# Reordering edits in the attention stage of a one-core transformer block: fill transfers spread over more turns, one GpSimd wait dropped, filler matmuls and two VectorE steps moved

## What is computed

```
xn = layernorm(x) * g_in
q  = xn @ Wq (16 heads of 64);  k, v = xn @ Wkv (one head, shared)
s  = q k^T / 8 + attn_bias[h];  causal mask; rows of the key mask; one extra "null" key per head
o  = softmax(s) v;  y = layernorm(o @ Wo) * g_out
n  = rmsnorm(y) * norm_w;  logits = n @ router^T + router_b
each of 16 experts takes its 512 best tokens: gelu(n W1 + b1) W2 + b2, weighted and scattered
out = x + that
```

## Time and profile before

| what | value |
|---|---|
| median of three executions | 1998.95 us (1996.95 to 2002.93) |
| the profiled execution | 2002.93 us, of which 2001.2 us lie between its first and last instruction |
| mean granted TensorE clock | 0.985 of full speed |
| PE busy | 1910.4 us (95%) |
| DVE, ACT, POOL busy | 1509.1, 1319.0, 1226.7 us |
| DRAM traffic | 139 GB/s over the span |

### The profile page before, as it was taken

One profiled execution on the slowest core, in us unless ns is written; L12 is line 12 of the kernel. 1 busy time (PEld: TensorE's weight loads), 2 busy tenths in 40 slices (PEclk: granted clock), 3 DMA queues, 4 the chain that ended last, 5 costly groups with the idle time before them and its releaser, 6 DMA issues.

```text
span 2001.2 us, 42090 instructions
## 1 busy us (share of the span) xinstructions
PE 1910.4 (95%) x12660; PEld 1702.7 (85%) x12660; DVE 1509.1 (75%) x2361; ACT 1319.0 (66%) x2624; POOL 1226.7 (61%) x1229
## 2 busy tenths in 40 slices
PE   4799999998789999999999999999999999999998
PEld 3678888877779898898999899898998889988897
DVE  5778887776887878777787877777787777777764
ACT  4667777754556666666676666767666666766664
POOL 3478888873057647565674757656574756657561
PEclk9899999998999999999999999999999999999999
DMA  6844444334743525254343525344352525434342
GB/s 247 320 139 128 125 131 139 106 97 171 231 107 112 138 100 142 95 147 106 125 125 112 142 95 142 97 140 123 113 147 90 152 87 150 106 122 120 121 126 44
DMA packets 90255, 263.14 MB, mean 131 GB/s; under 512 B 20593, under 2 KB 22353, under 8 KB 85073
## 3 DMA queue, kind: packets, MB, share of 16 engines
q1 hardware_dynamic: 70866, 211.44, 32.3%
q0 software_dynamic: 17024, 34.19, 9.0%
q10 hardware_dynamic: 2304, 16.78, 2.1%
HBM read 223.47 MB, written 55.60 MB: 139 GB/s over the span
## 4 chain that ended last, share of the span: by engine, by line
PE 69%; DVE 3%; ACT 2%; issue 1%; DMA 0%; POOL 0%; DVEq 0%; ACTq 0%; POOLq 0%
PE experts_b_a L2313 18%; PE experts_b_y L252 11%; PE experts_b_y L253 11%; PE experts_b_y L254 11%; PE experts_b_b L2313 9%; PE experts_b_c L2313 4%; PE experts_b_turn L2293 1%; ACT experts_h L1814 1%; DVE experts_x_lo L1967 1%; PE experts_b_c L2302 1%; PE experts_b_turn L2302 1%; PE experts_b_c L2391 0%; ACT experts_y_out L1748 0%; DVE experts_y_out L2005 0%; DVE experts_y_out L2103 0%
## 5 line engine op out<-in xcount | busy, mean ns | idle before, releaser
L252 PE MATMUL experts_b_y<-experts_w_hi,experts_h_hi 128*128 128x512 f32 x1024 | 406.3, 397 | 0.0
L1592 POOL TENSOR_TENSOR experts_s_raw<-experts_w_raw 128x256 f32<-128x256 f32 x128 | 147.7, 1154 | 421.7 <-DMA experts_w_raw<-in_w 410.7
L253 PE MATMUL experts_b_y<-experts_w_lo,experts_h_hi 128*128 128x512 f32 x1024 | 404.2, 395 | 0.0
L254 PE MATMUL experts_b_y<-experts_w_hi,experts_h_lo 128*128 128x512 f32 x1024 | 399.1, 390 | 0.0
L2313 PE MATMUL experts_b_a<-experts_x_hi,experts_w_hi 128*128 (+1 forms) x1024 | 290.2, 283 | 9.2 <-ACT experts_p_copy L1773 7.0
L2313 PE MATMUL experts_b_a<-experts_x_hi,experts_w_lo 128*128 (+1 forms) x1024 | 290.0, 283 | 0.0
L2313 PE MATMUL experts_b_a<-experts_x_lo,experts_w_hi 128*128 (+1 forms) x1024 | 289.9, 283 | 0.0
L254 PEld LDWEIGHTS experts_b_y<-experts_w_hi,experts_h_lo 128*128 128x128 f32 x1024 | 192.4, 188 | 43.3
L2313 PEld LDWEIGHTS experts_b_a<-experts_x_hi,experts_w_hi 128*128 128x128 f32 x1024 | 194.8, 190 | 29.5 <-issue 11.4
L252 PEld LDWEIGHTS experts_b_y<-experts_w_hi,experts_h_hi 128*128 128x128 f32 x1024 | 194.3, 190 | 24.0
L253 PEld LDWEIGHTS experts_b_y<-experts_w_lo,experts_h_hi 128*128 128x128 f32 x1024 | 194.3, 190 | 21.2
(11 more groups left out here) (378 smaller groups left out, 5564.7 us busy)
## 6 DMA issues: line engine op xcount, KB each, us to landing
experts_w_raw<-in_w SPq DMA_DIRECT2D x256, 512.0 KB, 3.3
bias<-in_bias SPq DMA_DIRECT2D x68, 256.0 KB, 4.1
xn_dram<-wq_hi ACTq DMA_DIRECT2D x16, 1024.0 KB, 10.5
spread_w<-weight_dram SPq DMA_DIRECT2D x32, 512.0 KB, 5.9
attend_q_x<-in_x SPq DMA_DIRECT2D x17, 256.0 KB, 2.8
attend_k_x<-in_x SPq DMA_DIRECT2D x17, 256.0 KB, 5.8
xn_dram<-rows_y_xn SPq DMA_DIRECT2D x17, 256.0 KB, 4.6
experts_b_sb<-in_b SPq DMA_DIRECT2D x16, 256.0 KB, 4.2
```

Source lines behind the costliest of these rows:

```text
L252: nc.tensor.matmul(out, lh, rh, start=first, stop=False)
L253: nc.tensor.matmul(out, lh, rl, start=False, stop=False)
L254: return nc.tensor.matmul(out, ll, rh, start=False, stop=last)
L1592: nc.gpsimd.tensor_tensor(s1, a21, a22, ALU.add).then_inc(s_done, 1)
```

## The change

Five edits in `attend`:

1. POOL no longer waits for `max_kept` between `key_root` and the second `add_new`.
2. The 16 fill transfers, which ACT issues in four groups of 4 behind `key_norm` in turns 0 to 3, are issued as 3 behind `query_norm` and 2 behind `key_norm` in turn 0, then 2 in each of the turns 1 to 5 and 1 in turn 6.
3. DVE makes `query_parts(j - 2, 1)` behind the two `out_parts` and not ahead of them.
4. DVE's `logits_elsewhere` moves, within the same turn of the drain, from behind `out_parts` to behind `out_rows(j - 6)`; the next steps there are `out_stats` of the last pair and the logits.
5. PE loses its filler groups of 13 and of 27 transposes in the last turns, and the group of 18 ahead of the last `rows_turned` becomes 36.

More of the change, by code:

```diff
@@ L627, in turn @@
                         key_root(j - 1)
-                    if on(-3):
-                        done(pool, max_kept, j - 3)
                     if on(-5) and not is_last(edge, on, -5):
@@ L753, in split_wq @@
                                          scale=keep["g_col"][:, k:k + 1]).then_inc(keep["hi_done"], 1)
-                filled = (0, 4, 8, 12, PIECES, PIECES, PIECES, PIECES)
                 def fill_pieces(first, last):
@@ L798, in turn @@
                         query_norm(j)
+                        if edge and j == 0:
+                            fill_pieces(0, 3)
                     if on(-1):
@@ L807, in turn @@
                         if edge:
-                            fill_pieces(filled[j], filled[j + 1])
+                            fill_pieces(3 + 2 * j, min(5 + 2 * j, PIECES))
                     if on(-1):
@@ L1005, in turn @@
                         carry = number(dve, j - 4, 6, 1)
-                    if on(-2):
-                        query_parts(j - 2, 1)
                     if on(-5):
@@ L1011, in turn @@
                         out_parts(j - 5, 1)
-                    if is_last(edge, on, -5):
-                        logits_elsewhere(j - 8)
-                        at = number(dve, j - 7, 5, NT)
+                    if on(-2):
+                        query_parts(j - 2, 1)
                     if on(-4):
@@ L1077, in turn @@
                         query_parts(j - 1, 0)
-                    if on(-7) and not is_last(edge, on, -5):
+                    if edge and not on(-4) and on(-5):
+                        logits_elsewhere(j - 8)
+                    if on(-7):
                         at = number(dve, j - 7, 5, NT)
@@ L1231, in turn @@
                         queries_turned(j - 1, 0)
-                    if is_last(edge, on, -5):
-                        keep_going(13, bank[0])
                     if on(-5) and not is_last(edge, on, -3):
@@ L1238, in turn @@
                         project(j - 5, out_bank(edge, on, -5))
-                    if is_last(edge, on, -6):
-                        keep_going(27, bank[0])
                     if on(-7):
@@ L1276, in turn @@
                         if is_last(edge, on, -6):
-                            keep_going(18, bank[0])
+                            keep_going(36, bank[0])
                         rows_turned(j - 6)
```

## The result

The changed kernel took 2012.36 us (median of 4 runs, 2008.14 to 2013.86) where the kernel before took 2000.20 beside it (4 runs): a ratio of 1.0058, 95% interval 1.0035 to 1.0081. It is slower by 0.6%, about 12 us, where 7.4 us less were forecast. The profiled execution after took 2010.12 us, its span 2008.4, at a mean granted clock of 0.986 (2002.93, 2001.2 and 0.985 before).

What follows compares the result with a forecast made beforehand. PE was taken as the bound, busy in experts and loop, with gains possible only in fill and drain. -8.1 - 4.2 + 4.9 = -7.4 us; 1991.5 forecast against the median 1998.95 (chance 0.50), range 1984 to 2000.

Steps and rivals of the forecast that it cites:

- In the loop POOL idles at it and PE doesn't notice: Attention loop: POOL's wait for `max_kept` costs PE nothing there, so no loop time was counted for dropping it.
- The drain step of edit 1, -4.2 us: First drain turn: POOL's steps move up 1.9 us and the low clock goes; -4.2 us, bounds 1.9 and 5.3.
- Edit 2, -8.1: Pipeline fill: fewer pieces per turn mean shorter ACT issuing and earlier bias landings; -8.1 us, bounds 2 to 12.2.
- the sum 1.5 + 2.7 + 1.5: Fill, turns 1 and 2: ACT issuing 1.5, landing 2.7, ACT issuing 1.5 us, 5.7 us gained.
- rival 1: Fill: the next releaser stands right behind, so the front gives only -2; total -1.3 us, 1997.7; chance 0.20.
- rival 3: Turns 4 to 6: pieces delay `spread_w`, PE loses 4.3 us in each, +12.9; total +7.9, 2006.9; chance 0.08.
- its 7.4: Turns 4 to 6: a loss of 2.4 us a turn, 7.4 in all, uses up the forecast gain.
- Edit 3 at nothing: DVE's swapped order: `qT_lo` comes 1.29 us later with 0.3 us to spare in turn 4; nothing gained or lost.
- Edits 4 and 5, +4.9,: End of attention: longer filler makes the last turn 3.6 us late, low clock adds 1.3; bounds 3.6 to 8.0.
- the 0.6 of the estimate: End: without the logits copy beside them POOL's small steps get 0.6 us faster, and `out_rows` as much earlier.
- rival 4: End: the filler runs at the low clock throughout, costing 8.0 us; total -4.3, 1994.7; chance 0.12.
- Rival 2: First drain turn: the clock falls again, so only 1.9 us is gained; total -5.1, 1993.9; chance 0.10.

Runs made afterwards that it cites:

- front_clear: Kernel before with 3 fill pieces ahead of the first turned query and the other 13 all in turn 6; ratio to before 1.0137.
- fill_late: Kernel before with the change's fill transfers, but from turn 3 on the pieces are issued at the end of ACT's turn, behind the `spread_w` load; 0.9978.
- wait_swap: Kernel before with only POOL's wait for `max_kept` dropped and `query_parts` moved behind `out_parts` on DVE; 1.0003.
- end_only: Kernel before with only the end changed: logits copy behind `out_rows`, 36 fillers in place of 13, 27 and 18; 1.0031.
- after_old_end: Kernel after with the end undone: logits copy and filler groups as before, the other three edits kept; 1.0024 to before.
- after_no_swap: Kernel after with `query_parts` put back ahead of `out_parts` on DVE, all other edits kept; 1.0054 to before.
- best: Kernel before with the fills of fill_late and the moved wait of wait_later, no swap, old end; 1995.55 us, 0.9978.
- after_wait_kept: Kernel after with POOL's wait for `max_kept` put back, all other edits kept; 1.0045 to before.
- wait_later: Kernel before with POOL's wait for `max_kept` moved one step later, behind the second `add_new` and ahead of the null products; 0.9994.
- fill_only: Kernel before with only the fill transfers changed, to groups of 3, 2, 2, 2, 2, 2, 2, 1; 1.0001.

## Why the prediction was wrong

By the ratios of the single edits the forecast of -7.4 us missed by some 19 us: edit 1 cost 4.4 us where -4.2 was forecast, edit 2 gave nothing where -8.1 was forecast, and edits 4 and 5 cost 6.2 where 4.9 was.

**Edit 1 is the first step that failed.** "In the loop POOL idles at it and PE doesn't notice" is right of the wait and wrong of its removal. I looked for what is queued behind the waiting instruction, and not at what POOL's operations would then run beside. The loop lost 4.7 us to it (turns of 24.3 us in which DVE was held for 3.5 to 3.6 us, beyond its slack). I had the rule for the port pair in hand for the end, and did not apply it here, though the diff moves two wide SBUF operations of POOL onto three small SBUF operations of DVE.

The drain step of edit 1, -4.2 us, failed in its mechanism as well. POOL's wait for `neg_max` is gone and PE is busy without a gap from 400 to 422 us, but its idle time only comes later and is not shorter. These windows are of the drain before (two) and after (one):

```profile
410.00:420.00 10.00, 7.76 (x54) 6.58 (x52) 6.50 (x14) 7.50 (x30) 6.46 (x9) 1.00 0.77 210
420.00:430.00 10.00, 9.15 (x38) 8.07 (x39) 7.46 (x13) 2.43 (x6) 8.69 (x10) 0.66 0.01 3
...
422.00:430.00 8.00, 4.47 (x33) 3.46 (x32) 6.20 (x14) 7.17 (x26) 4.73 (x8) 1.00 0.24 65
```

Between transposes 15 and 17 PE was idle for 3.1 us before and 4.4 after; what went away is the low clock, 6.8 us of that stretch before and none after. And the clock doesn't answer to the wait alone: in that stretch it fell in seven of the ten kernels that keep the wait (six times for 6.8 us) and in three of the seven that drop or move it (3.4 us each). From transpose 15 to the end, with the old end, kernels with the wait dropped or moved need 74.6 to 75.7 us, 75.2 in the mean of five, and those with the wait in its place 75.5 to 78.5, 77.0 in the mean of six (front_clear, 76.2, among them): 1.8 us, where 4.2 were forecast and 1.9 was the lower bound. Where the clock never fell in it, the two kinds need the same, 75.5 (fill_late) and 75.4 (wait_swap). Whether dropping the wait makes the low stretch rarer is not shown.

**Edit 2, -8.1, is the second, and was worth nothing** (1.0001). The landing times went as said (bias quarters 5.2 us), but the front gave 2 to 3 us up to the first transpose. Without any piece in turns 0 to 5 but the first three (front_clear) it gave 2.7 there and 4.6 at the fourth; these are single executions, and kernels with the same front scatter by 3 to 5. The waits for `sc` and `kT_lo` fell from 7.3 to 1.8 us, and the next releasers stood right behind, `pT_lo`, `q_n` and `q`, with 5.6 us more. The step that failed is the sum 1.5 + 2.7 + 1.5, which counts what leaves one chain as if no other ended beside it. That is rival 1. Then rival 3 came true as well, in turns 4 and 5: "I count nothing, since the edit also lets POOL free `spread_w` earlier" was wrong for an edit that puts 2 MB ahead of a load whose slack I had noted as none. `spread_w` was 3.1 and 3.5 us late and PE lost about 7 us, 3 and 4 in two turns, where the rival had 12.9 in three. That this is near the 7.4 at which the rival has the gain used up is chance: its 7.4 is the gain of all edits together, and the front had gained less.

**Edit 3 at nothing** held: 1.0007 alone, 1.0054 against 1.0058 in the change.

**Edits 4 and 5, +4.9,** had the right mechanism and the wrong size. Measured are 7.1 us (end_only) and 7.3 (after against after_old_end), within the bounds of 3.6 to 8.0. In end_only `out_rows` came 0.5 us earlier after the last weights than before (23.7 us against 24.2), near the 0.6 of the estimate, but the step from it to `out_stats` grew by 3.3 us and not by 2.5: the 0.85 us behind the logits were not foreseen. The fillers took 5.6 us, near the 5.3 forecast and not the 7.6 of rival 4; the logits ahead of them at the low clock, 0.8 us more, stood only in the upper bound. 4.9 + 1.0 (`out_stats` 2.8 late and not 1.8) + 0.3 + 0.8 = 7.0 us, which is what was measured.

**Rival 2** (low clock in the first drain turn) did not happen in the kernel after; it did, for 3.4 us, in after_no_swap, after_old_end and best.

By these terms, at the end of attention: front -3.0, +0.4 and +4.6 (late `spread_w`, and DVE held), loop +4.7 (edit 1), drain and end +4.5 (7.1 to 7.3 for edits 4 and 5, less 2 to 3 in which the drain was shorter, without a low clock between transposes 15 and 17), together +11.2. My range reached to 2000 and left this out, because edit 1 had no term with a plus sign and rival 3 was given 0.08.

Left open: why POOL reaches its add later when wait and swap are changed together; whether the clock in the drain depends on edit 1; and how much of after_wait_kept's total (1.0045, where its parts, fills 1.0001, swap 1.0007 and end 1.0031, add up to 1.0039) is the edits' interplay and how much is chance.

## What to carry to other kernels

A wait that seems idle can be what keeps two engines off a shared resource. Before dropping one, list the operations that would then overlap, and price each small one at the whole length of the long one beside it. Then add these prices up for one turn and compare them with the engine's slack in a turn: 2.3 us cost nothing here, 3.3 cost about 1. Moving the wait by one step spread the holds, and the loss was gone. A transfer that is taken out of one crowded place has to land in another: look for the next load without slack, and issue behind it (0.9978) rather than ahead of it (1.0001). When a trace shows a gain, look at whether it arose where the edit is: a stretch at the low clock that happens to be missing is worth as much as an edit here. When a stage waits for several producers in turn, the gain from speeding up one is bounded by the next, and a kernel that takes the suspect away altogether gives that bound in one run.

## What the runs showed of the hardware

A DVE operation of 0.17 us with both operands in SBUF, or an SBUF copy, lasted up to 2.40 us beside a POOL operation (after_old_end) and ended 0.03 us after it. It counts as busy time, not as a wait: no view of waits shows it, only the mean ns of a group does. `out_rows`, two multiplications over 512 columns with all operands in SBUF, went from 0.82 to 1.30 us in the mean (1.91 in wait_later) and ended 0.55 us after POOL's operation. And 512 KB loads issued 2.6 and 3.2 us behind two pieces of 1 MB on another queue kept their reader waiting for 3.1 and 3.5 us, while one issued 4.3 us ahead of such a piece kept it for 0.6 at most. The Trainium skill ("DMA: Bandwidth & Descriptors", Queues, rings and completion order) has the engines go round their queues a packet at a time. No trace here shows the turns of the packets, and the landings came in the order of issue: in turn 5 of fill_only the pieces landed at 131.7 and 135.1 us and the two halves of the load at 138.0 and 141.3, and in turn 4 of fill_late the load, issued first, landed at 116.2 and 118.6 and the pieces at 124.0 and 127.4.
